# Moving SyncE's work for the second mixture, and two pairs' normalising, inside the distance-attention stage

## What is computed

```python
# attention by distance (on the normalised x)
q = x @ Wq + bq;  k = x @ Wk + bk;  v = x @ Wv + bv
dist_sq = q_sq[:, :, None] + k_sq[:, None, :] - 2.0 * qk
attn = softmax(exp(-dist_sq));  out = (attn @ v) @ Wo + bo
# mixture of experts (on the normalised x)
logits = x.mean(axis=1) @ Wr
top_scores, top_idx = top_k(logits, 2);  weights = softmax(top_scores)
h = gelu(x @ W1[top_idx] + b1[top_idx])        # 256 -> 1024
out = sum(weights * (h @ W2[top_idx] + b2[top_idx]))
```

## Time and profile before

| | |
|---|---|
| median of 3 runs | 1647.84 us (1646.92 to 1650.32) |
| the profiled execution | 1648.53 us, of which the span of the profile is 1646.8 us |
| PE busy | 1592.7 us, 97% |
| DVE / ACT / POOL busy | 1074.5 / 986.0 / 357.6 us |
| mean granted TensorE clock | 0.994 of full speed |
| distance stage, from its first product to its last | about 860 to 1305 us |
| last mixture | about 1300 us to the end |

### The profile page before, as it was taken

How to read it: one execution, slowest core, us unless ns; L and a number is a source line. 1 busy time by engine, 2 the same in 40 slices (tenths; PEclk the granted TensorE clock), 3 DMA queues, 4 the chain that set the end, 5 groups by cost and what they waited for, 6 DMA issues and landing times.

```text
span 1646.8 us, 30646 instructions
## 1 busy us (share of the span) xinstructions
PE 1592.7 (97%) x11755; PEld 872.0 (53%) x11755; DVE 1074.5 (65%) x2159; ACT 986.0 (60%) x1260; POOL 357.6 (22%) x466
## 2 busy tenths in 40 slices
PE   6999999999999999999999999999998899999998
PEld 2222222222223666666665666666665566666666
DVE  7533454444335975786656689868997897577554
ACT  6999999999998433543335545555444543353322
POOL 3022122022022000110003644365443400011000
PEclk9999999999999999999999999999999999999999
DMA  4013235000030003011110001100001211411100
GB/s 136 20 27 116 75 116 169 20 15 20 20 110 14 14 14 116 14 21 20 20 20 14 1 2 20 20 14 2 1 1 39 74 18 27 129 26 33 33 14 26
DMA packets 96560, 65.52 MB, mean 40 GB/s; under 512 B 55888, under 2 KB 91295, under 8 KB 96415
## 3 DMA queue, kind: packets, MB, share of 16 engines
q1 hardware_dynamic: 96414, 63.55, 14.1%
HBM read 38.88 MB, written 4.19 MB: 26 GB/s over the span
## 4 chain that ended last, share of the span: by engine, by line
PE 71%; ACT 11%; issue 10%; DVE 6%; POOL 1%; SPq 0%; DMA 0%; ACTq 0%; DVEq 0%; POOLq 0%
ACT a_probs L782 10%; PE a_out L539 7%; PE f_ypsum L1051 7%; PE f_ypsum L1049 7%; PE f_ypsum L1050 7%; PE f_h L1049 7%; PE f_h L1050 7%; PE f_h L1051 7%; PE a_scores L918 4%; PE d_outs L1049 3%; PE d_outs L1051 3%; PE d_outs L1050 3%; PE d_banks L1049 2%; PE d_banks L1051 2%; PE d_banks L1050 2%
## 5 line engine op out<-in xcount | busy, mean ns | idle before, releaser
L782 ACT ACTIVATE a_probs<-a_scores 128x1024 f32<-128x1024 f32 x544 | 500.1, 1211 | 7.1 <-PE a_scores L918 7.0
L1412 ACT ACTIVATE f_gelu<-f_h,f_bcol,s_more 128x512 f32<-128x512 f32 x256 | 198.8, 777 | 406.7 <-PE f_h L1051 392.0
L539 PE MATMUL a_out<-a_probs,a_values 128*32 128x512 f32 (+3 forms) x2560 | 294.0, 540 | 6.6 <-ACT a_probs L782 5.5
L1467 DVE TENSOR_SCALAR f_hh<-f_gelu,f_gates_scaled 128x512 f16<-128x512 f32 x256 | 135.2, 528 | 184.3 <-ACT f_gelu L1412 183.6
L1925 ACT ACTIVATE d_score<-d_dist,d_nksq,s_more 128x512 f32<-128x512 f32 x128 | 104.1, 813 | 198.9 <-DVE d_dist L2070 197.1
L1051 PE MATMUL f_ypsum<-f_w,f_hl 128*128 128x256 f16 x768 | 209.3, 273 | 0.0
L1049 PE MATMUL f_ypsum<-f_w,f_hh 128*128 128x256 f16 x768 | 209.3, 273 | 0.0
L1050 PE MATMUL f_ypsum<-f_w,f_hh 128*128 128x256 f16 x768 | 209.3, 273 | 0.0
L1469 DVE SCALAR_TENSOR_TENSOR f_hl<-f_gelu,f_gates_scaled,f_hh 128x512 f16<-128x512 f32 x256 | 193.3, 755 | 9.1
L918 PE MATMUL a_scores<-a_moving,a_fixed 64*128 64x512 f16 (+3 forms) x1280 | 183.6, 353 | 9.8 <-ACT a_probs L782 3.7
L1962 POOL TENSOR_TENSOR distance_raw<-distance_raw,d_p 128x512 f32<-128x512 f32 x112 | 148.4, 1325 | 189.7 <-ACT d_p L1902 189.6
(11 more groups left out here) (258 smaller groups left out, 2701.2 us busy)
## 6 DMA issues: line engine op xcount, KB each, us to landing
f_raw<-in_L_ffn_W SPq DMA_DIRECT2D x16, 1024.0 KB, 7.6
f_raw<-in_L_ffn_W SPq DMA_DIRECT2D x24, 512.0 KB, 7.6
a_fixed<-a_moving SPq DMA_DIRECT2D x60, 96.0 KB, 2.3
x<-in_L_attn_a_x SPq DMA_DIRECT2D x7, 512.0 KB, 6.3
out<-x SPq DMA_DIRECT2D x7, 512.0 KB, 3.1
f_raw<-in_L_ffn_W SPq DMA_DIRECT2D x12, 256.0 KB, 4.4
a_fixed<-a_moving SPq DMA_DIRECT2D x60, 32.0 KB, 2.0
f_early_raw<-in_L_ffn_W SPq DMA_DIRECT2D x4, 256.0 KB, 3.4
```

The lines of the kernel that those rows point to most:

```text
L539: mm = pe.matmul(spare[32 * j:32 * j + 32, i % 2, skip:skip + w], values[:, G % 2, kt + tile, j, :], probs[:, u % UR, j % 2, col:col + w], ...
L782: act.activation(probs[:, u % UR], scores[:, 2 * (u % SR):2 * (u % SR) + 2, :], ACT.Exp, scale=HD ** -0.5)\
L1412: act.activation(gel[:, n % HR, :], hps[:, n % 2, :], ACT.Gelu, bias=mix.bcol[:, q, FT * e + j:FT * e + j + 1], scale=pr.scales.hidden)\
L1467: dve.tensor_scalar(hh[:, n % HR, :], gel[:, n % HR, :], gate, None, ALU.mult).then_inc(s_hh, 1)
```

## The change

Three edits:

1. In the distance stage SP reads the choice and starts the four bias DMAs after the transposes of pair 15, ahead of those of pair 16. The early weight DMAs come after the transposes of pair 16, ahead of those of pair 17.
2. Pairs 6 and 7 are normalised and split at steps 0 to 3 instead of 3 to 6 (`norm` 6 and `high` 6 at 0, `low` 6 and `norm` 7 at 1, `high` 7 at 2, `low` 7 at 3).
3. In the last mixture SP reads the choice first, waits for `banks_read` alone, starts the `W1` DMAs of the next two pieces, then waits for `all_read` and starts their two `W2` DMAs and the other four.

```diff
-            all_read(sp)
             if loaded < len(mix.pieces):
-                mix.load_weights(sp, 0, mix.chosen(sp, 0), range(loaded, len(mix.pieces)))
+                rest = range(loaded, len(mix.pieces))
+                chosen = mix.chosen(sp, 0)
+                banks_read(sp)
+                mix.load_weights(sp, 0, chosen, rest[:2], (0,))
+                all_read(sp)
+                mix.load_weights(sp, 0, chosen, rest[:2], (1,))
+                mix.load_weights(sp, 0, chosen, rest[2:])
+            else:
+                all_read(sp)
...
-        AT = {0: [("lengths", 1), ("project", 2, 0)],
-              1: [("values", 1), ("project", 2, 1)],
-              2: [("values", 2), ("lengths", 2), ("project", 3, 0)],
-              3: [("project", 3, 1), ("norm", 6)],
-              4: [("high", 6), ("low", 6), ("norm", 7)],
-              5: [("values", 3), ("lengths", 3), ("project", 4, 0), ("high", 7)],
-              6: [("project", 4, 1), ("low", 7)],
+        AT = {0: [("lengths", 1), ("project", 2, 0), ("norm", 6), ("high", 6)],
+              1: [("values", 1), ("project", 2, 1), ("low", 6), ("norm", 7)],
+              2: [("values", 2), ("lengths", 2), ("project", 3, 0), ("high", 7)],
+              3: [("project", 3, 1), ("low", 7)],
+              5: [("values", 3), ("lengths", 3), ("project", 4, 0)],
+              6: [("project", 4, 1)],
               7: [("lengths", 4)],
...
-            for p in range(6, TILES + 2):
+            def turn(p):
                 if p >= cols.RING:
                     sp.wait_ge(s_v, p - cols.RING + 1)
                     g = (p - cols.RING) // 2
                     sp.wait_ge(s_p, KD * (max(task["q", g], task["k", g]) + 1))
                 cols.turn(sp, BASE + p)
+
+            for p in range(6, TILES):
+                turn(p)
             chosen = mix.chosen(sp, 0, routing)
             mix.load_biases(sp, 0, chosen)
+            turn(TILES)
             sp.wait_ge(s_len, len(tasks))
             mix.load_weights(sp, 0, chosen, range(len(mix.early_raw)))
+            turn(TILES + 1)
```

More of the change, by code:

```diff
@@ L1147, in load_biases, with load_weights @@
             sp.dma_start(self.b2_rows[e:e + 1, :], pr.b2[bass.ds(n, 1)]).then_inc(self.s_braw, 16)
-    def load_weights(self, sp, q, chosen, pieces):
+    def load_weights(self, sp, q, chosen, pieces, which=(0, 1)):
         pr = self.pr
@@ L1156, in load_weights @@
             if q == 0 and (e, first) in self.early_raw:
-                to1, to2 = self.early_raw[e, first]
+                to = self.early_raw[e, first]
             else:
-                to1, to2 = self.raw1[:, e, :, units], self.raw2[:, e, 2 * first:2 * end, :]
-            sp.dma_start(to1, pr.W1[bass.ds(n, 1), :, units].rearrange("o (k p) f -> p (o k) f", p=P)).then_inc(self.s_raw[at][0], 16)
-            sp.dma_start(to2, pr.W2[bass.ds(n, 1), units, :].rearrange("o (j p) d -> p (o j) d", p=P)).then_inc(self.s_raw[at][1], 16)
+                to = self.raw1[:, e, :, units], self.raw2[:, e, 2 * first:2 * end, :]
+            of = (pr.W1[bass.ds(n, 1), :, units].rearrange("o (k p) f -> p (o k) f", p=P),
+                  pr.W2[bass.ds(n, 1), units, :].rearrange("o (j p) d -> p (o j) d", p=P))
+            for w in which:
+                sp.dma_start(to[w], of[w]).then_inc(self.s_raw[at][w], 16)
     def tanh(self, act, q, routing):
```

## The result

| | before | after |
|---|---|---|
| median | 1647.71 us of 4 runs (1646.92 to 1650.32) | 1636.12 us of 4 runs (1635.10 to 1637.01) |
| ratio | | 0.9933, 95% interval 0.9922 to 0.9944 |
| profiled execution, span, mean clock | 1648.53, 1646.8, 0.994 | 1637.01, 1635.3, 0.999 |

The change makes the kernel 0.67% faster. The forecast was 1636.4, and 1637.1 for the profiled execution's own time.

The account below looks back on a forecast made before the run. PE, busy 1592.7 of 1646.8 us, was taken as the bound, gains coming from its gaps and low clock. 7.7 + 3.7 + 0 = 11.4 us off 1648.53 gave 1637.1, or 1636.4 for the median; range 1633 to 1642.

Parts of the forecast that it names:

- DVE can follow by 7.93 us: Distance steps 117 and 118: DVE's waits of 7.16 and 0.77 us let it follow PE forward by 7.7 us.
- The terms of the chain: DVE and ACT before `lengths` of task 4: 3.7 us taken out, 2.9 put in, so 0.8 us sooner.
- a gap of 1.6 us should leave it up: PE before `lengths` of task 4: shortened gap keeps the clock at full speed, saving 2.9 us.
- Rival A: Step 7: clock falls all the same or the chain gains nothing; -1 to +1 us, time 1640.1; chance 0.25.
- the bound of 1.7: Last mixture's first weights: most the earlier loads could gain, PE's gap of 1.7 us; 0 was expected.
- B: Steps 1 to 3: moved pair work opens a new PE gap, costing 1 to 4 us, 1641 to 1645; chance 0.10.
- D: Dense steps 1 to 12: clock stays low some 22 us after a new gap, kernel slower; chance 0.03.
- E: Biases or SP still held until PE's turn, so the bias move gives nothing, 1640 to 1648; chance 0.04.
- C: All gains come, last mixture's earlier weights too: 7.7 + 6.0 + 1.7 = 15.4 us, time 1632.4; chance 0.06.

Follow-up runs that it names:

- edit2: Kernel before with only the new table that normalises and splits pairs 6 and 7 earlier; 1645.12 us, ratio 0.9985.
- shift: Kernel after, with parts 4 to 15 of the last mixture's weights all split one step sooner; 1635.57 us, ratio 0.9923.
- shift_no3: Kernel after, with parts 4 to 15 split one step sooner but without the earlier last-mixture weight loads; 1638.11 us, ratio 0.9948.
- part4: Kernel after, with only part 4 of the last mixture's weights split at step 0 instead of step 1; 1636.50 us, ratio 0.9928.
- edit1: Kernel before with only SP's new order of choice, bias DMAs, early weights and transposes; 1640.53 us, ratio 0.996.
- edit3: Kernel before with only the last mixture's two loads changed; 1647.92 us, ratio 1.0002.
- warm: Kernel before with unread products filling PE's two gaps, 24 before the biases and 11 before `lengths` of task 4; 1643.47 us, ratio 0.9974.
- bias_only: Kernel before with only the choice and bias DMAs moved ahead, early weights left behind both transposed pairs; 1639.33 us, ratio 0.9953.
- late: Kernel after, with PE's `lengths` of task 4 moved behind the scores of step 8; 1634.46 us, ratio 0.9918.
- best: Kernel after, with `lengths` of task 4 behind step 8's scores and weight parts 4 to 15 one step sooner; 1633.55 us, ratio 0.992.

## Why the prediction was right, and where it was only lucky

**Edit 1: right in mechanism and size.** The prediction had 5.71 us idle and 2.0 of slow work. DVE's distances in the profile of after, steps 116 to 118, and the clock there (columns as in the earlier trace rows):

```profile
1251.07 0.69 DVE L2083 SCALAR_TENSOR_TENSOR d_dist<-d_banks,d_qsq 128x512 f32<-128x512 f32 x1
...
1253.94 0.69 DVE L2083 SCALAR_TENSOR_TENSOR d_dist<-d_banks,d_qsq 128x512 f32<-128x512 f32 x1
...
1256.55 0.69 DVE L2083 SCALAR_TENSOR_TENSOR d_dist<-d_banks,d_qsq 128x512 f32<-128x512 f32 x1
```
```profile
1250.00:1260.00 10.00, 10.00 (x70) 6.66 (x69) 9.54 (x19) 4.53 (x8) 5.28 (x4) 1.00 0.23 59
```

From step 116 to 118 it takes 5.48 us; before it was 13.26 (1254.80 to 1268.06), so 7.78 are gone, against 7.7. Neither of the last two distances waits any more. PE is busy for all ten us at full clock, and DVE for 9.5 of them. So the step "DVE can follow by 7.93 us" held with little to spare: by these numbers, little more could have been won on PE before it met DVE.

**Edit 2: the gap right, the clock half right.** Idle time in the profile of after was 0.84 us at `values` (0.85 forecast) and 1.35 before `lengths` (1.6 forecast). The terms of the chain held too: against the first distance, that of step 1 came 0.64 us later than before (0.65 forecast), that of step 2 another 1.67 later (1.7), that of step 3 0.65 back (0.56), and `low` 7 put 1.11 between (1.1). The chain reached `lengths` 1.06 us sooner (0.8). POOL wasn't held up: its sum beside `low` 6 took 1.26 us, as its others do. Where the clock stayed up the edit gave 3.9 us against 3.7 (stretch 40.95 to 37.06 in edit2). But in after it fell. PE at the gap, and the clock behind it:

```profile
899.21 1.02 PE L1822 MATMUL d_misc<-ones,distance_raw 128*128 128x1 f32 x8 [1.35 <-POOL distance_raw L1959]
...
900.90 0.63 PE L1049 MATMUL d_banks<-d_queries,d_khi 128*128 128x512 f16 x1
```
```profile
899.00:900.00 1.00, 0.79 (x8) 0.82 (x9) 0.96 (x3) 0.86 (x2) 0.06 (x1) 1.00 0.00 0
900.00:901.00 1.00, 1.00 (x7) 0.49 (x7) 0.39 (x2) 0.47 (x1) 0.45 (x1) 0.78 0.00 0
901.00:902.00 1.00, 1.00 (x4) 0.34 (x3) 0.00 (x0) 0.00 (x0) 0.81 (x1) 0.50 0.00 0
...
904.00:905.00 1.00, 1.00 (x11) 0.90 (x10) 0.17 (x1) 0.48 (x1) 0.45 (x1) 1.00 0.00 0
```

The gap ended at 899.21, and the clock was still at 1.00 until about 900.6, when PE was at work again: the product begun at 900.90 took 0.63 us instead of 0.38. So the clock has to be read behind a gap as well as in it.

The same stretch in the profile of shift, whose gap is 1.36 us:

```profile
900.00:901.00 1.00, 1.00 (x6) 0.43 (x5) 0.13 (x1) 0.13 (x1) 0.80 (x1) 1.00 0.00 0
901.00:902.00 1.00, 1.00 (x10) 0.88 (x9) 0.77 (x2) 0.05 (x1) 0.47 (x1) 1.00 0.00 0
```

Of five profiled executions with a gap of 1.35 to 1.36 us at this place, the clock stayed at 1.00 in three (edit2, shift, shift_no3) and fell to 0.50 in two (after, part4). The step that failed is "a gap of 1.6 us should leave it up": it was argued from one gap of 1.73 us elsewhere at which it did, as if the length of the gap settled it. Rival A's mechanism thus took place, in two profiles of five, but not at its price, and the chain gained all the same. The clock was low for 3.4 us here (added up from the stretches, about 900.6 to 904.0) instead of the 6.8 behind before's gap of 3.06 us, so it costs 1.7 us (38.73 against 37.06) instead of 2.9, and edit 2 is still worth 2.2.

The price of the old gap was a matter of chance as well, which the prediction, with one profile, couldn't see. In before, edit1 and edit3 the clock was low for 6.8 us at this gap and cost 2.9 (40.95 against warm's 38.07). In bias_only the gap is the same, but the clock fell only 2 us behind its end and for 3.4 us, which cost 1.7 (39.78 against 38.07). PE and the clock in the profile of bias_only:

```profile
900.03 1.02 PE L1814 MATMUL d_misc<-ones,distance_raw 128*128 128x1 f32 x8 [3.06 <-POOL distance_raw L1951]
```
```profile
901.00:902.00 1.00, 1.00 (x7) 0.41 (x6) 0.96 (x3) 0.93 (x2) 0.00 (x0) 1.00 0.36 69
902.00:903.00 1.00, 1.00 (x5) 0.56 (x4) 0.59 (x3) 0.40 (x1) 0.52 (x1) 0.50 0.35 67
```

So what edit 2 is worth depends on the executions that are compared: 1.06 us by which the chain came sooner, and the difference of two prices of the clock, 2.9 or 1.7 before and 0 or 1.7 after. By the medians of before and edit2 it is 2.7 us.

That the same gap costs the clock in one execution and not in the next fits what the Trainium skill says ("TensorE: Matmul & The Clock Gate", Part 1: the window in which activity is judged runs free of the kernel). This case's trace agrees, with 0.50 and 1.00 behind gaps of 1.35 and 1.36 us.

**Edit 3: right.** 0.0 us, by the last column of the table, alone as well as in the change. The reason given (DVE is busy up to the low half and comes to it no sooner) was tested from both sides: with DVE's order moved PE's gap moved (part4, shift), and only then did the weights' DMA become what is late (shift_no3). In that other order, which the prediction didn't price, edit 3 is worth 3.6, above the bound of 1.7.

**The sum.** Forecast for the profiled execution: 7.7 + 3.7 + 0 = 11.4. Found: 7.8 + 2.2 + 0 = 10.0, and 1.5 more ahead of the change. The 1.5 us is the clock once more, near the very start of the program, where both kernels do the same. PE's first product behind a pause there and the next 2 us, before and then after:

```profile
23.65 1.01 PE L866 MATMUL a_scores<-ident,a_split_m 128*128 128x128 f16 x8 [1.94 <-DVE a_split_m L605]
```
```profile
24.00:26.00 2.00, 2.00 (x15) 0.60 (x12) 1.41 (x5) 0.00 (x0) 0.71 (x2) 0.50 0.00 0
```
```profile
23.65 0.61 PE L866 MATMUL a_scores<-ident,a_split_m 128*128 128x128 f16 x8 [1.94 <-DVE a_split_m L605]
```
```profile
24.00:26.00 2.00, 2.00 (x20) 0.63 (x18) 1.81 (x6) 0.38 (x1) 0.71 (x2) 1.00 0.00 0
```

The same instructions start at the same 23.65 us behind the same pause of 1.94 us, and the clock falls in one execution and not in the other. Nothing that an edit moves runs there. But there is only one profile of each kernel. The clock is low at this place in before, edit2 and edit3 and up in the other nine, and of the four kernels without edit 1 only warm is among those nine. That it is chance and not something that comes with edit 1 is therefore likely, not shown. The prediction compared with the one profile it had and didn't ask in which places that execution had been unlucky. For the profiled execution, 1637.01 against 1637.1, an overestimate of 1.4 and these 1.5 cancel; for the median, 1636.12 against 1636.4, something like it is likely, but the other executions have no profile. By the medians the edits alone give 7.3, 2.7 and 0, together 10.0, and the change 11.6; the intervals of edit1 and edit2 (4.4 to 8.9 and 1.0 to 4.0 us) leave room for the difference. That edit1 alone gave 7.3 and not 7.8 fits the 0.5 us that its profile lost where DVE and POOL meet.

**The other rivals.** B didn't come: the only new wait at steps 1 to 3 is the 0.84 us at `values`, and the clock stayed up. D and E are refuted by the stretches: the clock was low for 3.4 us and not for 22, and edit 1 gave all it could. C's time would have needed edit 3 to be worth something, which in this order it isn't.

## What to carry to other kernels

When PE is nearly always busy, price a gap twice, as idle time and as the slow work behind it, and read the second from the clock of the stretches behind it; but once a gap has become short, treat the slow work as a matter of odds, and judge one profile's stretches against another's, not against the forecast alone. Small DMAs that an engine will need should not be queued behind transposes that wait for something unrelated. A DMA started earlier gains nothing while the engine behind it has other work to do first: look whether that engine idled, and if it did not, change its order first.

## What the runs showed that was not expected

- The same gap of 1.35 to 1.36 us before `lengths` left the granted clock at 1.00 in three profiles and took it to 0.50 for 3.4 us in two. The executions' spread fits it: after's four are 1637.01 and 1636.72 us at a mean clock of 0.999, and 1635.10 and 1635.52 at 1.000. With the gap shortened (late) the spread was 0.3 us.
- Added up from stretches of 1 us over the whole span of all twelve profiles, and leaving out the last 3 us of a span, every low stretch of the clock lasted 3.4 us or 6.8 us and nothing between: 6.8 at the biases' gap (before, edit2, edit3); at `lengths` 6.8 in before, edit1 and edit3 and 3.4 in bias_only, after and part4; 3.4 in shift_no3 at its new gap and in the three profiles with a fall 24 us into the span. warm, late, shift and best have none. A low stretch of 3.4 us cost 1.5 to 1.7 us.
- The kernel before spreads over 6.7 us, 1643.66 (mean clock 0.997) to 1650.32 over all its executions. As the whole program runs the same instructions each time, and a mean clock lower by 0.001 is worth about 1.6 us of 1640, clock drops at different places explain most of it; that was read from the means and only in the profiled executions from the places.
- One such place is 24 us into the span, worth 1.5 us: low in the profiles of before, edit2 and edit3 (first stretch 869.1 to 869.3), up in the others (867.4 to 867.9). The two executions of best that are 1.5 us longer than its others fit it, but they have no profile, so it is not shown.
- Thirty-five more products made the kernel before 4.4 us faster by the medians (warm). In its profile the clock is never low, in that of before for 17 us; of the 6.2 us between the two profiles 1.8 lie ahead of the distance stage, where the products do nothing, and 4.4 behind.
- Two instructions of DVE and POOL that start within 0.03 us of each other went one way in ten profiles and the other way in two, and the second way cost 0.5 us of the kernel's time.
